# New step tables for attention and the four shared batches of an attention and mixture-of-experts kernel

## The reference

```python
x = x + _layernorm(attn(_layernorm(x)))       # x: 8 x 512 x 512, fp32
x = x + _layernorm(ffn(_layernorm(x)))
...
c_kv = x @ W_DKV + b_DKV;  c_q = x @ W_DQ + b_DQ        # latent 128
k_c, v_c, q_c = c_kv @ W_UK + b, c_kv @ W_UV + b, c_q @ W_UQ + b
k_r, q_r = (x @ W_KR + b) * pe, (x @ W_QR + b) * pe     # shared by the 16 heads
scores = concat(q_c, q_r) @ concat(k_c, k_r)^T / sqrt(32)
out = softmax(scores) @ v_c @ W_O + b_O
...
scores = sigmoid(x @ router_weight^T)                   # 16 experts
# best 2 of 4 groups by the sum of their two best, then the best 2 experts of them
routed = sum_e weight_e * relu(x @ w_up[e])^2 @ w_down[e]
shared = relu(x @ shared_up)^2 @ shared_down
```

## Time and profile before

| | us |
|---|---|
| median of 3 runs | 1635.28 (1633.22 to 1638.73) |
| the profiled execution, its own time | 1637.92 |
| its span, first to last instruction | 1636.1 |
| mean granted clock of TensorE | 0.969 |

### The profile page before, as it was taken

One profiled execution on the slowest core, in us unless ns is written; L12 is line 12 of the kernel. 1 busy time (PEld: TensorE's weight loads), 2 busy tenths in 40 slices (PEclk: granted clock), 3 DMA queues, 4 the chain that ended last, 5 costly groups with the idle time before them and its releaser, 6 DMA issues.

```text
span 1636.1 us, 21814 instructions
## 1 busy us (share of the span) xinstructions
PE 1518.9 (93%) x7006; PEld 1028.9 (63%) x7006; DVE 970.2 (59%) x1871; ACT 783.9 (48%) x1417; POOL 797.5 (49%) x820
## 2 busy tenths in 40 slices
PE   4799999999999999999998998894999999979997
PEld 3465656656556566565653776683666666657886
DVE  3566767676766667676666426831333333339998
ACT  2355566565665656656547452330222222255554
POOL 1177696776957778769678410002222222133341
PEclk9799999999999999999999999897999999989999
DMA  4757368475583764737842234207977777596773
GB/s 117 207 134 215 85 187 259 114 206 148 152 247 103 218 194 129 222 107 203 278 130 79 77 134 157 90 20 222 296 219 218 216 212 211 169 332 216 232 238 127
DMA packets 169415, 291.32 MB, mean 178 GB/s; under 512 B 20596, under 2 KB 72692, under 8 KB 163156
## 3 DMA queue, kind: packets, MB, share of 16 engines
q1 hardware_dynamic: 150280, 242.21, 48.9%
q0 software_dynamic: 12912, 41.82, 8.7%
q10 hardware_dynamic: 6112, 5.90, 1.2%
HBM read 154.07 MB, written 92.01 MB: 150 GB/s over the span
## 4 chain that ended last, share of the span: by engine, by line
PE 75%; DMA 8%; DVE 6%; SPq 4%; issue 3%; ACT 3%; POOL 2%; DVEq 0%; POOLq 0%; ACTq 0%
PE bank L113 13%; PE bank L729 9%; PE bank L775 8%; PE bank L798 8%; PE bank L707 7%; PE bank L628 6%; PE bank L614 6%; PE bank L633 5%; PE bank L644 5%; DMA a<-kq_scratch 4%; PE bank L653 2%; SPq L1753 2%; DMA kq_scratch<-a 1%; PE bank L787 1%; POOL a L1594 1%
## 5 line engine op out<-in xcount | busy, mean ns | idle before, releaser
L1594 POOL TENSOR_TENSOR a<-a 128x512 f32<-128x512 f32 x384 | 497.2, 1325 | 121.6 <-PE bank L653 65.0
L1404 ACT ACTIVATE a<-bank 128x512 f32<-128x512 f32 x512 | 298.0, 598 | 250.1 <-PE bank L633 216.6
L908 DVE TENSOR_REDUCE a<-bank 128x1 f32<-128x512 f32 x512 | 323.6, 680 | 65.3 <-PE bank L614 64.5
L113 PE MATMUL bank<-a 128*128 128x512 f32 (+1 forms) x864 | 238.8, 400 | 5.9 <-DVE a L854 4.0
L628 PE MATMUL bank<-a 128*128 128x512 f32 x512 | 222.6, 435 | 4.9 <-ACT a L1404 4.1
L614 PE MATMUL bank<-a 128*128 128x512 f32 x512 | 185.1, 430 | 25.6 <-DMA a<-kq_scratch 21.5
L633 PE MATMUL bank<-a 68*128 68x512 f32 x512 | 206.6, 403 | 1.1 <-ACT a L1394 0.2
L707 PE MATMUL bank<-c 128*128 128x512 f32 x768 | 185.8, 403 | 19.4 <-ACT c L1477 7.4
L113 PEld LDWEIGHTS bank<-a 128*128 128x128 f32 (+1 forms) x864 | 160.3, 188 | 48.2 <-issue 4.4
L707 PEld LDWEIGHTS bank<-c 128*128 128x128 f32 x768 | 148.8, 195 | 55.3 <-issue 8.8
L1663 POOL DMA_INDIRECT f<-h_scratch,f x79 | 74.9, 949 | 217.0 <-DMA f<-f 214.5
(11 more groups left out here) (185 smaller groups left out, 1753.7 us busy)
## 6 DMA issues: line engine op xcount, KB each, us to landing
a<-kq_scratch SPq DMA_DIRECT2D x192, 256.0 KB, 5.9
kq_scratch<-a SPq DMA_DIRECT2D x32, 1024.0 KB, 4.1
a<-a SPq DMA_DIRECT2D x80, 256.0 KB, 5.4
f<-f SPq DMA_DIRECT2D x316, 64.0 KB
yp_scratch<-f SPq DMA_DIRECT2D x79, 256.0 KB, 3.2
a<-in_L_attn_x SPq DMA_DIRECT2D x15, 1024.0 KB, 9.1
x_scratch<-a SPq DMA_DIRECT2D x8, 1024.0 KB, 7.2
h_scratch<-a SPq DMA_DIRECT2D x8, 1024.0 KB, 13.0
```

Of the source, the lines that this page charges most:

```text
L113: t = e.matmul(out, a[n], b[n], start=n == 0 and m == 0, stop=n == len(ah) - 1 and m == 2)
L908: e.tensor_reduce(K.mx[:, i, j:j + 1], K.MX[n % 3][:], AX.X, ALU.max).then_inc(Z.max, 1)
L1404: e.activation(K.pt[:, n % NP, :], K.SC[n % 2][:], ACT.Exp, scale=SCALE).then_inc(Z.exp, 1)
L1594: e.tensor_tensor(K.acc[:, j, :], a, K.pt[:, n % NP, :], ALU.add).then_inc(Z.acc, 1)
```

## The change

Only the numbers in the two tables change, no function and no instruction. Of the lines that change, those on which the text below rests:

```diff
 FIRST_STEP = {
...
-        "prepare": (19,),
-        "early": (16, 16, 16, 17, 17, 17, 17, 18, 18, 19, 19, 19, 20, 20, 20, 20, 20, 20, 20, 20, 21, 22, 22, 22, 22, 23),
-        "late": (22, 23, 23, 23, 24, 24, 24, 24, 24, 24, 24, 24, 24, 24, 24, 24, 24, 24, 24, 24, 24, 24, 24, 24, 24, 24, 25, 25, 25, 25, 25, 25, 25, 26),
-        "weights": (43, 45, 47), "invert": (33, 34, 34, 35, 55, 55, 55, 56, 57)}
+        "prepare": (29,),
+        "early": (13, 13, 14, 14, 14, 14, 14, 15, 16, 17, 17, 18, 20, 20, 20, 20, 20, 20, 20, 21, 27, 28, 29, 31, 33, 35),
+        "late": (22, 22, 22, 22, 22, 22, 22, 22, 22, 22, 22, 23, 23, 23, 24, 24, 25, 25, 25, 25, 25, 25, 27, 27, 27, 27, 28, 28, 28, 29, 30, 30, 30, 36),
+        "weights": (44, 52, 56), "invert": (33, 33, 35, 35, 44, 44, 45, 45, 49)}
...
```

More of the change, by code:

```diff
@@ L146 @@
 FIRST_STEP = {
-        "rest": (1, 1, 2, 3, 2, 2, 3, 3, 3, 5, 4, 5, 8, 10, 6, 7, 8, 9, 8, 9, 9, 10, 11, 10, 10, 11, 11, 11, 11, 11, 11, 11, 12, 14),
-        "prepare": (19,),
-        "early": (16, 16, 16, 17, 17, 17, 17, 18, 18, 19, 19, 19, 20, 20, 20, 20, 20, 20, 20, 20, 21, 22, 22, 22, 22, 23),
-        "late": (22, 23, 23, 23, 24, 24, 24, 24, 24, 24, 24, 24, 24, 24, 24, 24, 24, 24, 24, 24, 24, 24, 24, 24, 24, 24, 25, 25, 25, 25, 25, 25, 25, 26),
-        "weights": (43, 45, 47), "invert": (33, 34, 34, 35, 55, 55, 55, 56, 57)}
-STEP = {"split up": (7, 11, 15, 20, 23, 27, 34, 39), "split h": (36, 43, 43, 44), "last values0": 9, "total0": 8, "invert0": 9,
[11 rows of a table removed]
+        "rest": (2, 2, 2, 3, 2, 2, 2, 3, 3, 5, 4, 5, 5, 7, 5, 6, 9, 9, 4, 9, 9, 9, 11, 9, 9, 9, 10, 10, 10, 10, 10, 10, 11, 13),
+        "prepare": (29,),
+        "early": (13, 13, 14, 14, 14, 14, 14, 15, 16, 17, 17, 18, 20, 20, 20, 20, 20, 20, 20, 21, 27, 28, 29, 31, 33, 35),
+        "late": (22, 22, 22, 22, 22, 22, 22, 22, 22, 22, 22, 23, 23, 23, 24, 24, 25, 25, 25, 25, 25, 25, 27, 27, 27, 27, 28, 28, 28, 29, 30, 30, 30, 36),
+        "weights": (44, 52, 56), "invert": (33, 33, 35, 35, 44, 44, 45, 45, 49)}
+STEP = {"split up": (4, 13, 17, 22, 25, 29, 36, 41), "split h": (38, 39, 42, 43), "last values0": 9, "total0": 8, "invert0": 5,
[11 rows of a table added]
 def beside_order(u):
```

## The result

| | before | after |
|---|---|---|
| median of 5 runs each on one chip, us | 1636.11 | 1628.07 (1624.27 to 1631.91) |
| ratio, 95% interval | 1 | 0.9951 [0.993, 0.9971] |
| span of the profiled execution, us | 1636.1 | 1630.1 |

A forecast was written before the change was run, and what follows sets the result against it. PE, busy 93% of the span, was taken as the bound: its own work plus its waits. Terms -5.4 - 10.2 + 1.6 + 2.5 + 1.4 - 9.0 + 3 = -16.1 us gave 1619 us, range 1605 to 1630.

The forecast's parts named there:

- Placing: Third shared batch: placing in pieces removes PE's 7.38 us wait and 2.8 of slow clock after it; -10.2 us.
- Turning: End of attention: transposes of h move before batch 0's last down projection, so PE waits for h; +1.6 us.
- One-hots: Fourth shared batch: PE waits for the second late group, +2.5; small matmuls move ahead of the last down projection, +1.4.
- Gap: Last down projection to first expert matmul: 23.5 us shrinks to 14.5, weights being issued earlier; -9.0 us.
- The rival of a gap that moves: Before the experts: weights still land beside fetch and moves, only 1.8 us of the gap go; 1626 us, chance 0.13.
- the 19.5 us: Gap before the experts if fetch shares with remaining weights and moves stand behind them; -4.0 in place of -9.0.
- Totals: Before the totals in the shared batches: choice ends near 1001, so 4.0 us wait and 1.4 slow stretch go; -5.4.
- Attention: Wait before each fourth unit's tops grows 0.7 in six or seven batches, partly offset; +3 us, between -12 and +12.
- the slower rival: Attention: stack late in all seven batches, PE's clock falling each time, 27 us against 19; 1643 us, chance 0.07.

The follow-up runs named there:

- late_only: The kernel before with only the new places of the placing (the new "late" entries); ratio 0.9929 to the kernel before.
- shared_only: The new FIRST_STEP with the old STEP, the shared batches' half of the change alone; ratio 0.9894 to the kernel before.
- both_back: The changed kernel with tops2 and the entries turn23, k3, q3 and tops3 set back as before; ratio 0.9907 to the kernel before.
- best_a: Changed kernel with new tops3 entries, every third unit's r projection at step 8, VectorE's first choice pieces later; 1607.11 us, ratio 0.9829 to the kernel before.
- the second execution: The changed kernel run again unedited in a second sitting; medians 1626.55 against 1630.06 us, ratio 0.9974 to the kernel before.
- best_b: best_a with the last four one-hot groups spread one, two, one after the fourth shared batch's first three down projections; ratio 0.9836 to the kernel before.
- the two halves of the change: The kernel before with only the shared batches' new table, ratio 0.9894, and with only attention's new table, ratio 1.0022.
- onehots_only: The kernel before with only the new places of the one-hots and of the weights of experts 7 to 10; ratio 0.9985.

## Why the prediction was right in kind and wrong in size

The forecast was -16.1, and the result is -8. The waits that it names went or came as it says: no wait of L738 or L707, one of 2.23 us between the one-hot groups, the weights 11 us before the end, a gap of 13.2 us, and stack waits of 1.9 to 3.5 us in every batch. What failed is the size of three terms, one of which I had put at nothing. Term by term:

- **Placing, -10.2: right.** The 96 up matmuls of the third batch take 21.92 us where they took 31.9, and late_only gave 9.4 us in its shared batches alone.
- **Turning, +1.6: right.** PE now waits 0.37 us for L1347 among the turns, and the whole comes to 1.0.
- **One-hots, +2.5 and +1.4: right, at its upper bound.** A wait of 2.23 us, 1.8 of slow clock behind it, and 1.4 of small matmuls ahead of the end: 5.4 us in place of 3.9. I had priced the drop of the clock only in the bound; in three of the twelve executions with this wait it does not come.
- **Gap, -9.0: right.** 23.3 became 13.2. The rival of a gap that moves is excluded. So is the 19.5 us that I worked out beside the Trainium skill's rule on queues, since I had taken the weights to be still in the way when the moves are issued, and they had landed.
- **Totals, -5.4: mis-sized, about -2.** The wait at L738 and its slow clock went, but the waits for L977 grew from 0.47 to 2.39 us, with 1.5 of slow clock behind them (not in every execution: shared_only and both_back have the waits without it). The step that failed is "from there VectorE needed 24.3 us ... now it leaves gaps and ends near 1001". Against the start of the shared batches the choice began 2.6 us earlier and ended only 1.0 earlier. The wait at L738 went mainly because PE came there 4.5 us later, held up by turning and by the two waits for L977. These I had not looked for. The first comes from L993: moved ahead, it stands waiting for its data and holds up what is queued behind it, and best_a took 1.0 us of that wait away by letting two L977 go first. The second comes from pieces of the choice between two L977. I had asked only when the choice would end.
- **Attention, +3: mis-sized.** The chain that I named (two tops ahead of the r projection, less work ahead of the wait) is the right one: both_back undoes these and the loss is gone. What failed is the price, "+0.7 in each of six or seven batches", and the credit against it. The wait grew by 0.7 a batch as said (17.1 to 23.1 us), but in most batches PE's clock now falls at it, which I had written down only for the slower rival. So the first seven fourth units are 14.2 us longer in all (10.8 in the second execution), and not 4.5; and the first seven third units are 7.7 us shorter, a credit that I had put at 1.5. The executions with the new table took 910.2, 910.3, 909.0 and 905.9 us, those with the old one 904.7, 904.2, 907.4 and 898.4: +5.2 on the mean.
- **Experts, not in the sum: +2.9 on the mean.** The step that failed is the silent one, that a shorter gap is kept in full. Before the change two tiles were turned and the moves of four were under way when PE began; now it is one tile and 10 moves, while the DMA engines are full (a share of 1.03 from 1128 to 1172 us). best_b agrees from the other side: with its gap 3.9 us longer it starts with two tiles in hand, and the experts are 2.2 us shorter.

The shared batches and the gap together gave 16.1 us in place of the 19.1 forecast. With the means for the other two stages the stages sum to -16.1 + 5.2 + 2.9 = -8.0. That this meets the first sitting's difference of medians to a tenth is chance: the second sitting gave -3.5, and the two halves of the change, each alone, -13.8 together.

## What to carry to other kernels

When a stretch ahead of a stage that starts on DMA gets shorter, ask how much that stage had fetched ahead in the time: part of the gain comes back there. When a wait for a transfer is moved forward in an in-order queue, move only the request, and leave the instruction that consumes it where the data are there. And price a wait on TensorE with the slow stretch that may come with it: here that stretch was as dear as the wait's growth, or dearer.

## What the runs showed of the hardware that I had not expected

The same wait is followed by a slow clock in one execution and not in the next, so two executions of one kernel differ by several microseconds. In the fifth batch of the first execution of the changed kernel:

```profile
569.45 0.97 PE L614 MATMUL bank<-a 128*128 128x512 f32 x3 [2.01 <-DMA a<-kq_scratch]
...
571.00:576.00 5.00, 5.00 (x22) 3.23 (x20) 3.81 (x7) 3.06 (x5) 0.00 (x0) 0.73 1.04 365
```

and in the second:

```profile
568.25 0.97 PE L614 MATMUL bank<-a 128*128 128x512 f32 x3 [1.77 <-DMA a<-kq_scratch]
...
571.00:576.00 5.00, 5.00 (x29) 2.28 (x31) 4.76 (x8) 3.68 (x7) 0.00 (x0) 1.00 1.07 417
```

The waits differ by 0.24 us, the granted clock is 0.73 against 1.00 over the next 5 us, and the unit takes 28.65 against 26.95 us. Likewise both_back, whose two waits for L977 (1.25 and 0.96 us) are those of the changed kernel's second execution (1.22 and 0.96, with 13.02 us for the 49 matmuls behind them), runs these matmuls at full clock:

```profile
985.25 11.41 PE L729 MATMUL bank<-c 128*128 128x512 f32 x49 [0.96 <-DVE c L977]
```

That is 1.6 us less. The wait of 2.23 us for the second late one-hot group is the same to 0.01 us in twelve executions, and 24 matmuls behind it take 7.30 to 7.35 us in nine of them and 5.71 in three (onehots_only, best_a, both_back). The length of the wait alone does not tell whether the clock falls; what does, no run here shows. So an edit that takes a few tenths of a microsecond from a wait can bring several times that or nothing, and one profile is not enough to price it.
